# The first chunk of a gated delta-rule recurrence, begun inside the triangular solve ahead of it

## The chip, the cores and the metric

One core of a Trainium2 chip runs the kernel. The metric is the device time of one execution in microseconds; the kernel before was run three times, and its median is the time before. On the core, TensorE (PE in the profile) multiplies matrices, VectorE (DVE) and ScalarE (ACT) do the elementwise work and copy results out of PSUM, GpSimd (POOL) does some small work, and SyncE (SP) issues most of the transfers. Engines wait for each other by semaphores.

## What is computed

The reference is one transformer layer over 2048 tokens of width 512: a layer norm, then a gated delta-rule attention and a feed-forward part whose weights are spline-interpolated. Only the attention's recurrence matters here; per token and head (6 heads, keys of 64, values of 128):

```python
def _step(S, xs):
    qt, kt, vt, gt, bt = xs
    S = S * jnp.exp(gt)[..., None, None]
    pred = jnp.einsum('bhk,bhkv->bhv', kt, S)
    delta = (vt - pred) * bt[..., None]
    S = S + jnp.einsum('bhk,bhv->bhkv', kt, delta)
    return (S, jnp.einsum('bhk,bhkv->bhv', qt, S))
```

The kernel doesn't go token by token. For a chunk of 128 tokens all deltas U come from one triangular system: U = W (V - gamma K S), with W an inverse that doesn't depend on the state S, and K S the product of the chunk's keys with the state at its start.

## The kernel before, in words

The function `attend` computes the attention, `feed` the feed-forward part behind it. `attend` goes over 4 supersteps of 512 tokens, each of 4 chunks of 128 tokens (NCH = 4). One superstep has a part that needs no state (`local`: projections, convolutions, scores, and at its end `solve`, which puts together the inverse W of each chunk) and a part that does (`recur`, once for each chunk). On TensorE, `recur` of superstep r stands behind `solve` of superstep r, and the projections of superstep r+1 behind that.

Every engine has its own program, written out by hand; what keeps them in step are the eight PSUM banks. `bank_uses` (line 163) lists every use of every bank in order. `claim` (547) makes TensorE wait until the use before in this bank has been read out; `filled` (528) makes a reader wait until TensorE has written it; `ready` (533) makes anyone wait until the reader is done. The change leaves `bank_uses` as it is.

`solve` on TensorE (650) is a pipeline of seven steps, k = 0 to 6. Step k holds, in this order: a transpose of values (`v_transposes(k + 1)`, for k = 1 to 4), X of chunk k (line 660), Y and Z of chunk k-1 (670, 676), and, interleaved, X2 of chunk k-2 (691) and Z2 of chunk k-3 (696). So the fifth step (k = 4) has the last transpose, Y and Z of chunk 3, X2 of chunk 2 and Z2 of chunk 1; the sixth has X2 of chunk 3 and Z2 of chunk 2; the seventh has Z2 of chunk 3 alone. All Z2 lie in bank 6, all X2 in bank 7, so the Z2 of one chunk can be made only once that of the chunk before has been copied out.

VectorE's `solve` (1006) copies out X (1012), Y (1019), Z (two instructions, 1024) and Z2 (1031), in that order within a step. ScalarE (1309 to 1315) goes through, for c = 0 to 3: `v_tokens(c + 2)`, which copies a transposed block of values out into V in four pieces (1246), and the copy of X2 of chunk c (1314). Its last `v_tokens` (for head 5) thus stands behind the copy of X2 of chunk 2.

`recur` on TensorE (710) makes, for chunk c: KS, the keys times the state, in two halves of three heads (706); U, with the inverse, in two halves (722), once VectorE's `right_sides` (1034, the six instructions of line 1041) has made V - gamma K S out of KS; QS, the queries times the state (706 too, in banks 6 and 7); dS, the state's increment (733); AU (740). VectorE's `state` (1051) then updates S, for which the next chunk's KS waits. KS lies in banks 2 and 3, U in banks 4 and 5. A matmul of float32 shows as two records.

## Time and profile before

| | us |
|---|---|
| median of 3 runs | 1062.36 (1059.04 to 1064.06) |
| span of the profiled execution, first to last instruction | 1047.6 |
| TensorE busy | 904.7 |
| VectorE busy | 632.2 |
| ScalarE busy | 456.8 |
| GpSimd busy | 331.9 |
| mean granted clock of TensorE, share of full speed | 0.922 |

The profiled execution's whole duration isn't given, only its span; the median stands 14.8 us above that. The span is one hardware-profiled execution; the runs are others. A row of a timeline gives the start and the duration of an instruction, or of several like ones in a row (x12), and in brackets how long its engine had been idle and who released it. The part with the feed-forward network starts at about 700 us and isn't touched.

### The profile page before, as it was taken

The numbers are of one execution on the slowest core, as the hardware profiler recorded it, in microseconds if no ns is written. First come the engines' busy times: TensorE is split into PE (matmuls) and PEld (weight loads), VectorE is DVE, ScalarE is ACT, GpSimd is POOL, SyncE is SP. The second block draws the span as 40 slices with busy tenths as digits, with TensorE's granted clock in tenths as the row PEclk, the third lists the DMA queues.
The fourth block names the chain that finished last, engine by engine and source line by source line (L and its number), as shares of the span: only waits on it lengthen the run. The fifth ranks groups of instructions, "written<-read, shape, count | busy, mean of one in ns | idle before, by whom it ended". The sixth has DMA issues, their size and how long they took to land. (4 is left out here: it accounts for less than half of the span.)

```text
span 1047.6 us, 16055 instructions
## 1 busy us (share of the span) xinstructions
PE 904.7 (86%) x5976; PEld 527.2 (50%) x5976; DVE 632.2 (60%) x1447; ACT 456.8 (44%) x1038; POOL 331.9 (32%) x348
## 2 busy tenths in 40 slices
PE   3788298989798989798989798667699999999888
PEld 1453187555486555486555486322344444444333
DVE  5889656676656676656676645359892291390530
ACT  3645335445635535635435634245771170260420
POOL 2477601165701265701265701079060000000000
PEclk9999689989979989979989979967899999999999
DMA  6322310101410101410101300160552102101101
GB/s 203 136 61 58 67 36 21 71 1 31 81 52 21 71 1 31 81 52 21 71 1 31 81 12 21 45 225 0 208 174 71 50 1 80 41 0 40 40 21 41
DMA packets 70543, 61.61 MB, mean 59 GB/s; under 512 B 48059, under 2 KB 52028, under 8 KB 70470
## 3 DMA queue, kind: packets, MB, share of 16 engines
q1 hardware_dynamic: 62526, 41.42, 13.9%
q0 software_dynamic: 4224, 13.37, 4.0%
q10 hardware_dynamic: 3720, 5.85, 1.6%
q8 instruction: 45, 0.74, 0.3%
q14 instruction: 28, 0.23, 0.1%
HBM read 38.08 MB, written 23.13 MB: 58 GB/s over the span
## 5 line engine op out<-in xcount | busy, mean ns | idle before, releaser
L1924 ACT ACTIVATE sg<-pg 128x512 f32<-128x512 f32 x64 | 37.6, 590 | 147.6 <-PE pg L1825 147.5
L2040 DVE SCALAR_TENSOR_TENSOR yr<-pd,yr 128x512 f32<-128x512 f32 x16 | 11.1, 691 | 146.4 <-PE pd L1836 146.4
L1834 PE MATMUL pd<-dw,it 128*128 128x512 f16 x256 | 97.1, 379 | 1.5 <-DVE it L2035 1.5
L1835 PE MATMUL pd<-dw,it 128*128 128x512 f16 x256 | 97.1, 379 | 0.0
L1836 PE MATMUL pd<-dw,it 128*128 128x512 f16 x256 | 97.1, 379 | 0.0
L1734 POOL DMA_DIRECT2D yr<-y_attn x16 | 8.7, 544 | 239.4 <-DMA out<-yr 239.4
L559 PE MATMUL bank<-x_hi,w_hi 128*128 128x512 f16 x192 | 73.7, 384 | 2.7 <-DVE x_lo L866 1.5
L559 PE MATMUL bank<-x_lo,w_hi 128*128 128x512 f16 x192 | 73.5, 383 | 0.0
L559 PE MATMUL bank<-x_hi,w_lo 128*128 128x512 f16 x192 | 73.3, 382 | 0.0
L559 PE MATMUL bank<-w_hi,x_hi 128*128 128x384 f16 x128 | 44.4, 347 | 23.9 <-ACT gate L1207 15.4
L1407 POOL TENSOR_TENSOR rn<-t,mhalf 128x6 f32<-128x6 f32 x16 | 22.6, 1415 | 128.1 <-DVE t L1066 128.1
L1798 PE MATMUL pf<-fx_hi,b_hi 128*128 128x512 f16 x128 | 52.3, 408 | 0.7 <-DVE f L1989 0.7
L2031 DVE TENSOR_TENSOR hh<-sg,pu 128x512 f32<-128x512 f32 x64 | 43.9, 687 | 14.3 <-ACT sg L1924 9.6
L909 DVE SCALAR_TENSOR_TENSOR cv<-raw,taps,cv 128x512 f32<-128x512 f32 x72 | 52.3, 791 | 0.0
L1799 PE MATMUL pf<-fx_lo,b_hi 128*128 128x512 f16 x128 | 52.1, 407 | 0.0
L1800 PE MATMUL pf<-fx_hi,b_lo 128*128 128x512 f16 x128 | 51.4, 402 | 0.0
L706 PE MATMUL bank<-S,kq 64*128 64x128 f32 x384 | 48.0, 321 | 4.0 <-DVE BA L1062 3.7
L950 DVE SCALAR_TENSOR_TENSOR BA<-bank,cj,eg 128x256 f32<-128x256 f32 x96 | 39.0, 474 | 18.1 <-PE bank L639 15.1
L989 DVE TENSOR_TENSOR bank<-bank,tin 96x60 f32<-96x60 f32 (+32 forms) x184 | 46.6, 281 | 2.3
L1340 ACT ACTIVATE junk<-BA 128x128 bf16<-128x128 f32 x96 | 28.6, 298 | 42.5 <-DVE BA L1062 42.4
L995 DVE TENSOR_TENSOR tin<-tin,bank 96x60 f32<-96x60 f32 (+32 forms) x184 | 45.4, 272 | 2.2
L706 PEld LDWEIGHTS bank<-S,kq 64*128 64x128 f32 x384 | 41.4, 215 | 9.0 <-issue 7.2
(249 smaller groups left out, 2300.7 us busy)
## 6 DMA issues: line engine op xcount, KB each, us to landing
xb<-in_x SPq DMA_DIRECT2D x4, 1024.0 KB, 5.7
xr<-in_x SPq DMA_DIRECT2D x16, 256.0 KB, 2.8
y_attn<-xr SPq DMA_DIRECT2D x16, 256.0 KB, 2.5
down_rows<-dn SPq DMA_DIRECT2D x4, 1024.0 KB, 7.8
yr<-y_attn POOLq DMA_DIRECT2D x16, 256.0 KB, 2.8
out<-yr SPq DMA_DIRECT2D x16, 256.0 KB, 2.0
xn_hi<-x_hi POOLq DMA_DIRECT2D x4, 512.0 KB, 3.1
xn_lo<-x_lo POOLq DMA_DIRECT2D x4, 512.0 KB, 4.5
```

What stands on the lines that cost most here:

```text
L559: ins = nc.tensor.matmul(out, a, b, start=first and i == 0, stop=last and i == 2)
L706: ins = nc.tensor.matmul(ps[:, 128 * (h // 2):128 * (h // 2) + 128], kq[rows, h // 2, which, CH * c:CH * c + CH], P.S[rows, h // 2, :], st ...
L909: ins = v.scalar_tensor_tensor(out=out, in0=src, scalar=w, in1=out, op0=ALU.mult, op1=ALU.add)
L989: done_to[k] = step(v.tensor_tensor(prod, row.unsqueeze(2).broadcast_to([NINST, n, c1 - c0]), tv[:, j, c0:c1].unsqueeze(1).broadcast_to([N ...
L995: done_to[k] = step(v.tensor_tensor(rest, rest, prod, ALU.subtract))
L1798: nc.tensor.matmul(ps[:], f_h, x_hi[:, hb, :], start=hb == 0, stop=False)
L1799: nc.tensor.matmul(ps[:], f_h, x_lo[:, hb, :], start=False, stop=False)
L1800: ins = nc.tensor.matmul(ps[:], f_l, x_hi[:, hb, :], start=False, stop=hb == HB - 1)
L1834: nc.tensor.matmul(ps[:], it_hi[:, i, tok], dw[:, i, 0, :], start=i == 0, stop=False)
L1835: nc.tensor.matmul(ps[:], it_hi[:, i, tok], dw[:, i, 1, :], start=False, stop=False)
L1836: ins = nc.tensor.matmul(ps[:], it_lo[:, i, tok], dw[:, i, 0, :], start=False, stop=i == IB - 1)
L2031: v.tensor_tensor(hh[:, i % 2, :], sg[:, i % 2, :], pu[i % 2][:], ALU.mult).then_inc(h_ready, 1)
```

## The change

KS of chunk 0 is made inside `solve`, its first half ahead of the fifth step's Y, its second half behind the fifth step's Z. VectorE makes the right sides of chunk 0 in its own fifth step, behind the copies of Z and ahead of the copy of Z2 of chunk 1, and waits for the last values (`("vtr", NV - 1)`) first. U of chunk 0 is made behind the sixth step. `recur` of chunk 0 begins with QS. Chunks 1 to 3 are as before; the functions `state_product` and `right_sides` are only moved up, and `solved_sides` is the part of `recur` that makes U.

```diff
+            def solved_sides(s, c):
+                ready(pe, ("Z2", c), s)
+                for hf in range(2):
+                    ps, f = claim(("U", c, hf), s)
+                    ready(pe, ("KS", c, hf), s)
+                    for h in range(hf, NH, 2):
+                        ins = nc.tensor.matmul(ps[:, 128 * (h // 2):128 * (h // 2) + 128], W[:, ch(c, h), :], Rr[:, h, :], start=True, stop=True)
+                    ins.then_inc(f, 1)
+
             def solve(s):
...
+                    if k == NCH:
+                        state_product(s, 0, "KS", 0, 0)
                     c = k - 1
                     if 0 <= c < NCH:
...
+                    if k == NCH:
+                        state_product(s, 0, "KS", 0, 1)
                     c, c2 = k - 2, k - 3
...
+                    if k == NCH + 1:
+                        solved_sides(s, 0)
 
             def recur(s, c):
                 if c >= 1:
                     ready(pe, ("dS", c - 1), s)
-                for hf in range(2):
-                    state_product(s, c, "KS", 0, hf)
-                if c >= 2:
-                    project_out(s, c - 2)
-                ready(pe, ("Z2", c), s)
...
+                    for hf in range(2):
+                        state_product(s, c, "KS", 0, hf)
+                    if c >= 2:
+                        project_out(s, c - 2)
+                    solved_sides(s, c)
                 for hf in range(2):
                     state_product(s, c, "QS", 1, hf)
...
                             ins = v.tensor_scalar(W[r:r + SUB, mine, r + SUB:r + 2 * SUB],
                                                   heads64(ps, slice(r, r + SUB))[:, :, SUB:], -1.0, None, ALU.mult)
                         ins.then_inc(d, 1)
+                    if k == NCH:
+                        ready(dve, ("vtr", NV - 1), s)
+                        right_sides(s, 0)
                     c = k - 3
                     if 0 <= c < NCH:
                         filled(dve, ("Z2", c), s)
...
             def recur(b, c, following=None):
-                right_sides(b, c)
+                if c >= 1:
+                    right_sides(b, c)
                 if following is not None and c == 0:
                     ln_tile_stats(following)
```

## Rows read from the trace of the kernel before

Rows 7 and 8 are tables by stretch; their columns are: stretch, its length, then busy time and count for TensorE, its weight loads, VectorE, ScalarE and GpSimd, then the granted TensorE clock as a share of full speed, the busy share of the transfers' engines and GB/s.

**Rows 1.** From the page: span, busy time of the engines, TensorE clock in 40 slices

```profile
span 1047.6 us, 16055 instructions
...
PE 904.7 (86%) x5976; PEld 527.2 (50%) x5976; DVE 632.2 (60%) x1447; ACT 456.8 (44%) x1038; POOL 331.9 (32%) x348
...
PEclk9999689989979989979989979967899999999999
```

**Rows 2.** Timeline of ACT, last solve: start, duration, line, operation

```profile
614.27 0.48 ACT L1314 ACTIVATE X2s<-bank 64x384 f32<-64x384 f32 x1 [1.01 <-PE bank L691]
614.78 1.14 ACT L1246 ACTIVATE V<-bank,nk 128x128 f32<-128x128 f32 x4
```

**Rows 3.** Timeline of DVE, last solve, and the right sides of the first chunk

```profile
613.76 0.71 DVE L1024 TENSOR_SCALAR W<-bank 32x192 f32<-32x192 f32 x2 [0.17 <-PE bank L676]
614.50 0.55 DVE L1031 TENSOR_SCALAR W<-bank 64x384 f32<-64x384 f32 x1
...
618.84 1.64 DVE L1041 SCALAR_TENSOR_TENSOR BA<-bank,ngam,V 128x128 f32<-128x128 f32 x6 [0.52 <-PE bank L706]
```

**Rows 4.** Timeline of PE, last solve, from its first step to its seventh

```profile
598.36 1.55 PE L660 MATMUL bank<-Tbd,BA 64*64 64x64 f32 x24 [4.04 <-DMA Tbd<-t_blocks]
599.83 1.11 PE L647 MATMUL bank<-ident,vT 128*128 128x128 f32 x4
...
602.21 1.38 PE L670 MATMUL bank<-eg,W 64*64 64x64 f32 x11
...
605.38 0.92 PE L660 MATMUL bank<-Tbd,BA 64*64 64x64 f32 x24
...
615.26 0.24 PE L691 MATMUL bank<-T,BA 64*64 64x64 f32 x1 [1.03 <-DVE W L1031]
...
616.83 0.91 PE L696 MATMUL bank<-W,X2s 64*64 64x64 f32 x12 [0.65 <-DVE W L1031]
```

**Rows 5.** Timeline of PE, last superstep, first chunk

```profile
617.66 1.77 PE L706 MATMUL bank<-S,kq 64*128 64x128 f32 x12
619.85 2.90 PE L722 MATMUL bank<-BA,W 128*128 128x128 f32 x12 [0.42 <-DVE BA L1041]
622.68 2.24 PE L706 MATMUL bank<-S,kq 64*128 64x128 f32 x12
624.85 1.55 PE L733 MATMUL bank<-BA,ktok 128*64 128x128 f32 x12
626.33 2.63 PE L740 MATMUL bank<-BA 128*128 128x128 f32 x12
```

**Rows 6.** Timeline of PE, last superstep, second chunk

```profile
628.88 1.72 PE L706 MATMUL bank<-S,kq 64*128 64x128 f32 x12
630.87 1.70 PE L722 MATMUL bank<-BA,W 128*128 128x128 f32 x12 [0.26 <-DVE BA L1041]
632.49 1.26 PE L706 MATMUL bank<-S,kq 64*128 64x128 f32 x12
...
635.55 0.88 PE L733 MATMUL bank<-BA,ktok 128*64 128x128 f32 x12
636.36 1.61 PE L740 MATMUL bank<-BA 128*128 128x128 f32 x12
```

**Rows 7.** One microsecond each, last superstep: busy time by engine, then clock, DMA

```profile
618.00:619.00 1.00, 1.00 (x11) 1.00 (x10) 0.48 (x2) 0.00 (x0) 0.00 (x0) 0.63 0.00 0
...
628.00:629.00 1.00, 1.00 (x7) 0.88 (x7) 0.56 (x1) 0.32 (x2) 0.00 (x0) 0.75 0.00 0
```

**Rows 8.** Same columns, 14 us from the sixth step of each solve

```profile
145.00:159.00 14.00, 11.50 (x102) 10.34 (x104) 7.99 (x24) 4.47 (x15) 1.02 (x1) 0.76 0.00 1
301.00:315.00 14.00, 12.55 (x96) 11.21 (x96) 7.30 (x24) 4.07 (x13) 0.09 (x1) 0.63 0.00 1
458.00:472.00 14.00, 12.62 (x96) 11.21 (x96) 7.54 (x24) 4.00 (x13) 0.40 (x1) 0.63 0.00 1
```

**Rows 9.** The line that evacuates Z2: who waited for it, in total us, times

```profile
  PE bank L691: 4.2, 4
```

More of the change, by code:

```diff
@@ L648, in v_transposes, with state_product @@
                 ins.then_inc(f, 1)
+            def state_product(s, c, name, which, hf):
+                ps, f = claim((name, c, hf), s)
+                for h in range(hf, NH, 2):
+                    rows = slice(DK * (h % 2), DK * (h % 2) + DK)
+                    ins = nc.tensor.matmul(ps[:, 128 * (h // 2):128 * (h // 2) + 128], kq[rows, h // 2, which, CH * c:CH * c + CH],
+                                           P.S[rows, h // 2, :], start=True, stop=True)
+                ins.then_inc(f, 1)
[4 more added lines that the diff above has]
+                    ready(pe, ("KS", c, hf), s)
+                    for h in range(hf, NH, 2):
+                        ins = nc.tensor.matmul(ps[:, 128 * (h // 2):128 * (h // 2) + 128], W[:, ch(c, h), :], Rr[:, h, :], start=True, stop=True)
+                    ins.then_inc(f, 1)
             def solve(s):
@@ L699, in solve @@
                                 ins.then_inc(f2, 1)
-            def state_product(s, c, name, which, hf):
-                ps, f = claim((name, c, hf), s)
-                for h in range(hf, NH, 2):
-                    rows = slice(DK * (h % 2), DK * (h % 2) + DK)
-                    ins = nc.tensor.matmul(ps[:, 128 * (h // 2):128 * (h // 2) + 128], kq[rows, h // 2, which, CH * c:CH * c + CH],
-                                           P.S[rows, h // 2, :], start=True, stop=True)
-                ins.then_inc(f, 1)
+                    if k == NCH + 1:
+                        solved_sides(s, 0)
             def recur(s, c):
@@ L712, in recur @@
                     ready(pe, ("dS", c - 1), s)
-                for hf in range(2):
-                    state_product(s, c, "KS", 0, hf)
-                if c >= 2:
-                    project_out(s, c - 2)
-                ready(pe, ("Z2", c), s)
-                for hf in range(2):
-                    ps, f = claim(("U", c, hf), s)
-                    ready(pe, ("KS", c, hf), s)
-                    for h in range(hf, NH, 2):
-                        ins = nc.tensor.matmul(ps[:, 128 * (h // 2):128 * (h // 2) + 128], W[:, ch(c, h), :], Rr[:, h, :], start=True, stop=True)
-                    ins.then_inc(f, 1)
+                    for hf in range(2):
[3 more added lines that the diff above has]
+                    solved_sides(s, c)
                 for hf in range(2):
@@ L998, in invert_blocks, with right_sides @@
                 step(v.tensor_copy(bin_[:].rearrange("p (c i) -> p c i", c=SUB), tin[:].rearrange("p (i c) -> p c i", i=SUB)))
+            def right_sides(s, c):
+                for hf in range(2):
+                    u = ("KS", c, hf)
+                    filled(dve, u, s)
+                    ps, d = out_of(u)
+                    for h in range(hf, NH, 2):
+                        ins = v.scalar_tensor_tensor(out=Rr[:, h, :], in0=ps[:, 128 * (h // 2):128 * (h // 2) + 128],
+                                                     scalar=ngam[:, ch(c, h):ch(c, h) + 1], in1=V[:, c, h, :],
+                                                     op0=ALU.mult, op1=ALU.add)
+                    ins.then_inc(d, 1)
             def heads3(ps):
@@ L1032, in solve @@
                                         ALU.mult).then_inc(d, 1)
-            def right_sides(s, c):
-                for hf in range(2):
-                    u = ("KS", c, hf)
-                    filled(dve, u, s)
-                    ps, d = out_of(u)
-                    for h in range(hf, NH, 2):
-                        ins = v.scalar_tensor_tensor(out=Rr[:, h, :], in0=ps[:, 128 * (h // 2):128 * (h // 2) + 128],
-                                                     scalar=ngam[:, ch(c, h):ch(c, h) + 1], in1=V[:, c, h, :],
-                                                     op0=ALU.mult, op1=ALU.add)
-                    ins.then_inc(d, 1)
             def state(s, c):
```

## The prediction

> **What bounds the kernel now.** I read the page first, then the granted clock, then the timelines of the three engines around one solve. TensorE is busy for 86% of the span and its clock dips once in each superstep [rows 1]; the mean hides that the stretch which the change touches isn't a stretch of full matrices. It is a relay: TensorE makes a small product, VectorE or ScalarE copies it out, and TensorE's next step waits for that copy. In the last solve VectorE finishes the masked copies of Z at 614.47 and the copy of Z2 for chunk 1 at 614.50 + 0.55 = 615.05 [rows 3]; TensorE stands idle for 1.03 us and starts the sixth step at 615.26, put down to that very copy; the seventh waits 0.65 us for the next one [rows 4]. All four solves do it: TensorE waited for that line 4.2 us in 4 waits, 1.05 each [rows 9]. Behind the solve come, on TensorE one after the other, the key products KS (617.66), the product U with the inverse (619.85), the query products QS (622.68), the state's increment dS (624.85), AU (626.33) and the next chunk's KS (628.88) [rows 5, 6]. I use the start of that last one as the finish line: what it moves by, each superstep moves by, since every later chunk hangs on this one and the feed part starts only behind the last.
>
> The second thing to see is the clock. It is at its upper level (2.4 GHz) through the solve, falls to 1.2 GHz in the microsecond from 618 (0.63, so at about 618.3) and is back in the one from 628 (0.75, so at about 628.5) [rows 7]. The three other supersteps show the same dip (means of 0.76, 0.63 and 0.63 over 14 us) [rows 8]. U, QS, dS and AU of the first chunk take 2.90, 2.24, 1.55 and 2.63 us in it [rows 5] against 1.70, 1.26, 0.88 and 1.61 in the second chunk at the upper level [rows 6].
>
> **The change, part by part.** No instruction is added or taken away; twelve matmul records (KS) and six vector operations (1.64 us) per superstep move ahead, and one wait is added. No DMA and nothing on GpSimd or SyncE moves. I walk the last superstep, as its rows are complete.
>
> *KS into the fifth step.* KS costs 1.26 us at the upper clock (the like-shaped QS) [rows 6] where it took 1.77 [rows 5]. But it stands ahead of the product X2 of chunk 2, so X2 and Z2 of that step end 1.26 us later. ScalarE's copy of X2 moves from 614.27 to 615.53 [rows 2]. This price is certain: the products run in the order in which they are written.
>
> *The new wait.* VectorE's right sides need V of chunk 0 for all heads, so it now waits for the last V transposes to be copied out. On ScalarE that copy (four pieces, 1.14 us) stands behind the X2 copy: 614.78 before [rows 2], so 615.53 + 0.51 = 616.04 now, done at 617.18. This is the crux. TensorE made that transpose at the head of the fifth step; it is ScalarE's order that keeps it back.
>
> *What is queued behind the wait.* On VectorE, first the six right sides: 617.24 to 618.88 (1.64 us) [rows 3]. Then the copy of Z2 of chunk 1, which was ready all along: to 618.88 + 0.55 = 619.43 instead of 615.05. TensorE's sixth step claims the same bank and waits for it. With the old hand-over (615.05 to 615.26, 0.21) it starts at 619.64 instead of 615.26: 4.4 us later, and TensorE idles for about 4.1 us where it idled for 1.03.
>
> *What is given back.* The sixth step's 24 small products, then U at once (its inputs are long ready), then the seventh step, whose wait is now hidden under U, then QS. Gone are the old KS between solve and U (617.66 to 619.85, 2.2 us with the 0.42 us wait for the first right sides [rows 5]) and the 0.65 us. New is a wait ahead of QS: it needs the bank of the last Z2, which VectorE can empty only behind the seventh step: 0.04 + 0.55 + 0.2, about 0.8 us.
>
> *At which clock.* The clock already falls at 618.3 with gaps of 1.03 and 0.65 us before it; with one of 4.1 us in the same place I take it to fall at the same time, so that everything from the sixth step on runs at the lower level. Durations there: 24 small products 1.47 (598.36 to 599.83) against some 0.75 at the upper one (0.92 less the tail of the last); the twelve of Z2, between 0.83 (616.83 to 617.66, mostly at the upper level) and 1.38 (eleven of the like-shaped Y at the lower), take 1.25 [rows 4, 5]. So: sixth step 619.64 to 621.1; U 2.83 to 623.95; Z2 to 625.2; wait to 626.0; QS 2.17 to 628.2; the clock rises at 628.5 as before, in dS, which ends at 629.15; AU about 1.55 to 630.7. KS of chunk 1 starts at 630.7 instead of 628.88: 1.8 us later. For four supersteps, taken as equal: 7.3 us.
>
> The clock's own terms are the unknown ones; their bounds, by the same walk. With the upper level throughout: sixth step to 620.4, U (1.62) 622.0, Z2 (0.83) 622.85, wait 623.65, QS (1.19) 624.85, dS (0.81) 625.65, AU (1.55) 627.2: a gain of 1.7 us. With a rise only behind AU: QS 628.2, dS (1.48) 629.7, AU (2.8) 632.5: a loss of 3.6 us. I take the value between, whose fall and rise are those of the rows.
>
> *A rule against the trace.* The profile shows short gaps behind nothing but vector copies, and the clock down 1.6 us after the second [rows 4, 7]. The Trainium skill ("TensorE: Matmul & The Clock Gate", the section "Loop structure matters more than you think") says that a VectorE copy out of PSUM between bursts of matmuls doesn't cost the engine its warmth, and that a long wait for a DMA does. Were that so here, the upper-level walk would hold (rival 3 below); in this trace the clock fell behind just such copies.
>
> *Switches of the array's shape.* The moved products put 64x128 tiles between 64x64 ones, twice more per superstep. Going from Z2 (64x64) to KS shows 0.07 us of overlap and no idle [rows 4, 5]: between 0 and 0.2 us each, taken as 0. The skill's "TensorEngine Tiling (Array Packing)", section "Key Properties", says that a change of tiling mode drains the engine; by it the sum would be longer, by less than the bound here.
>
> The sum is made on the profiled execution. Its span is 1047.6 us [rows 1]; its whole duration isn't given; the median of the three runs lies 14.8 us above the span, which I leave as it is. 1062.4 + 7.3 = 1069.7, so 1070.
>
> **The rivals.**
> 1. *Late rise.* The longer gap also keeps the clock down through AU: four times 3.6, 14.4 us: 1077. For it: the gap is four times as long, and a second one of 0.8 us follows. Against: U, then at 128x128, keeps TensorE dense for 2.8 us.
> 2. *Early rise.* The clock comes back ahead of QS, near 625.5: QS 1.19 to 627.2, dS 628.0, AU 629.55, so 0.7 us later per superstep: 1065. For it: the first superstep's dip is the shortest (mean 0.76) [rows 8].
> 3. *The clock stays up: faster.* The inserted KS keeps TensorE dense in the fifth step, and the copies' gap doesn't bring the clock down before U is through. Price: minus 1.7 four times, 6.8 us: 1056. The point from which it decides is whether U is still at 2.4 GHz. Against: all four dips of today follow shorter gaps.
> 4. *The wait costs nothing.* If the V copy were done when VectorE asks for it (by 615.10, the end of the Z copies of today plus the 0.63 us of the first KS half), the right sides would end at 616.8, Z2's copy at 617.35, and TensorE would start the sixth step at 617.6, 2.3 us later instead of 4.4; the walk then ends 0.3 us ahead of today's at the lower clock: 1061. Against: ScalarE's order, by which the copy can't begin before X2 of chunk 2 is out.
>
> **How the numbers follow.** Forecast 0.60; late rise 0.13; early rise 0.14; clock stays up 0.07; wait free 0.06. The predicted time is the likeliest case's, 1070. Its own range, with the runs' spread of 5 us (1059.0 to 1064.1), is 1066 to 1074. For eight in ten I go down past the early rise to 1062, the edge of the free wait, and up to the late rise, 1077; outside lie the stay-up case and tails. About 0.5% (5.3 us) is what a measurement of this kernel tells from no change: the line is at 1067.7. Of the forecast case three quarters and more lie above it (0.48), of the late rise all (0.13): slower 0.62 with a little of the early rise. Faster by 0.5% needs the clock up nearly throughout: 0.05. The same: 0.33.
>
> **What would show it.** In the changed profile, right sides (line moved into the solve) should start 3 us after the Z copies end, with the V copy as the releaser; TensorE's sixth step should show about 4 us idle ahead of it; no gap before U; 0.8 us before QS; granted clock at 1.2 GHz from U on in all four dips. The forecast is wrong if TensorE's gap is under 2 us, if U runs in 1.7 us, or if the dip ends before QS. The sum is mis-sized where the next KS starts by other than 1.8 us later than now, counted from the start of the solve's fifth step.

## The result, and the profile after

| | before | changed |
|---|---|---|
| median of the timed runs, us | 1063.2 (4 runs, 1059.0 to 1065.8) | 1074.3 (4 runs, 1072.6 to 1076.3) |
| ratio to before | | 1.0138 (95%: 1.0100 to 1.0177) |
| the same on another chip (29 and 6 runs), us | 1046.5 | 1063.4, ratio 1.0159 (1.0127 to 1.0190) |
| span of the profiled execution, us | 1047.6 | 1071.9 |

The change makes the kernel slower, as forecast, but by more: 11.1 us between the medians (16.8 on the other chip) where the sum had 7.3. The profiled execution of the changed kernel took 1073.5 us for a span of 1071.9, so only 1.6 us lie around a span; the 14.8 us between the span and the median of before were no fixed part: the profiled execution of before was simply quicker than the timed ones, in the feed part, as further looks show below. The ratio on record, 1.0138, stands for 14.7 us, twice the sum, and is a little higher than that of the medians, 1.0104; the four runs listed for the kernel before don't show why. Ratios rest on fast runs alone: runs more than 1.5% above the fastest of their kernel are left out, which were one of 1504.3 us at a granted clock of 0.556 (right sides behind Z2) and two of the kernel before without its feed part.

The page of the changed kernel, in the lines of [rows 1]:

```profile
span 1071.9 us, 16059 instructions
...
PE 915.2 (85%) x5976; PEld 527.2 (49%) x5976; DVE 627.5 (59%) x1447; ACT 457.7 (43%) x1038; POOL 327.2 (31%) x348
...
PEclk9989689989889979999989889767889999999999
```

TensorE, last superstep: start, duration, line, operation. Line 655 makes KS and QS, 690 Y, 696 Z, 713 X2, 665 U, 718 Z2, 742 dS, 749 AU.

```profile
617.48 0.93 PE L655 MATMUL bank<-S,kq 64*128 64x128 f32 x6
618.34 0.85 PE L690 MATMUL bank<-eg,W 64*64 64x64 f32 x11
...
619.09 0.86 PE L696 MATMUL bank<-W,eg 64*64 64x64 f32 x23
619.88 0.93 PE L655 MATMUL bank<-S,kq 64*128 64x128 f32 x6
...
625.68 0.34 PE L713 MATMUL bank<-T,BA 64*64 64x64 f32 x1 [4.03 <-DVE W L1055]
...
627.16 2.93 PE L665 MATMUL bank<-BA,W 128*128 128x128 f32 x12
630.02 1.01 PE L718 MATMUL bank<-W,X2s 64*64 64x64 f32 x12
631.67 1.26 PE L655 MATMUL bank<-S,kq 64*128 64x128 f32 x12 [0.64 <-DVE W L1055]
632.87 0.88 PE L742 MATMUL bank<-BA,ktok 128*64 128x128 f32 x12
633.67 1.60 PE L749 MATMUL bank<-BA 128*128 128x128 f32 x12
635.42 1.51 PE L655 MATMUL bank<-S,kq 64*128 64x128 f32 x12
```

These answer [rows 4, 5]. KS stands ahead of Y (617.48) and behind Z (619.88). The sixth step begins at 625.68 after 4.03 us of idle time, released by VectorE's copy of Z2 (line 1055), where it was 1.03 us. U starts behind the sixth step with no gap and takes 2.93 us, at the lower clock. QS waits 0.64 us for the last Z2, then takes 1.26 us, and dS 0.88: the upper clock again.

VectorE and ScalarE in the same stretch, answering [rows 3] and [rows 2]:

```profile
620.00 0.71 DVE L1045 TENSOR_SCALAR W<-bank 32x192 f32<-32x192 f32 x2 [0.17 <-PE bank L696]
623.38 1.64 DVE L1016 SCALAR_TENSOR_TENSOR BA<-bank,ngam,V 128x128 f32<-128x128 f32 x6 [2.66 <-ACT V L1259]
624.93 0.54 DVE L1055 TENSOR_SCALAR W<-bank 64x384 f32<-64x384 f32 x1
...
631.07 0.55 DVE L1055 TENSOR_SCALAR W<-bank 64x384 f32<-64x384 f32 x1 [3.24 <-PE bank L718]
```

```profile
621.69 0.49 ACT L1327 ACTIVATE X2s<-bank 64x384 f32<-64x384 f32 x1 [3.04 <-PE bank L713]
622.20 1.14 ACT L1259 ACTIVATE V<-bank,nk 128x128 f32<-128x128 f32 x4
```

The Z copies end at 620.71. The right sides (line 1016) start at 623.38 after 2.66 us of idle time, released by ScalarE's copy of V; that copy starts only behind the copy of X2 (621.69). Z2 of chunk 1 comes last, done at 625.47. TensorE's clock (stretch, length, busy times of five engines, then the clock), answering [rows 7]:

```profile
623.00:624.00 1.00, 0.00 (x0) 0.00 (x0) 0.62 (x3) 0.34 (x2) 0.00 (x0) 0.73 0.00 0
630.00:631.00 1.00, 1.00 (x13) 0.88 (x12) 0.00 (x0) 0.49 (x1) 0.00 (x0) 0.86 0.00 0
```

It falls in the gap itself, at about 623.5, and is back at about 630.3, behind U: 6.8 us at 1.2 GHz where it was 10.2.

### The profile page after: what moved, and what is told of

Read it like the earlier page. It is cut to its first block and busy times, and to the rows that moved or that the text cites. A ratio compares the mean times of both kernels' runs of the same rounds, so it can differ in the third digit from the quotient of the medians.

```text
span 1071.9 us, 16059 instructions
## 1 busy us (share of the span) xinstructions
PE 915.2 (85%) x5976; PEld 527.2 (49%) x5976; DVE 627.5 (59%) x1447; ACT 457.7 (43%) x1038; POOL 327.2 (31%) x348
## 3 DMA queue, kind: packets, MB, share of 16 engines
q1 hardware_dynamic: 62526, 41.42, 13.6%
## 5 line engine op out<-in xcount | busy, mean ns | idle before, releaser
L2053 DVE SCALAR_TENSOR_TENSOR yr<-pd,yr 128x512 f32<-128x512 f32 x16 | 11.1, 692 | 148.1 <-PE pd L1849 148.1
L559 PE MATMUL bank<-w_hi,x_hi 128*128 128x384 f16 x128 | 44.6, 348 | 21.1 <-ACT gate L1220 12.6
L2044 DVE TENSOR_TENSOR hh<-sg,pu 128x512 f32<-128x512 f32 x64 | 43.9, 688 | 22.3 <-ACT sg L1937 11.8
L655 PE MATMUL bank<-S,kq 64*128 64x128 f32 x384 | 43.4, 288 | 8.9 <-DVE BA L1074 5.9
L559 PE MATMUL bank<-w_hi,x_lo 128*128 128x384 f16 x128 | 44.7, 349 | 0.0
```

Of the source, the lines that this page charges most:

```text
L559: ins = nc.tensor.matmul(out, a, b, start=first and i == 0, stop=last and i == 2)
L655: ins = nc.tensor.matmul(ps[:, 128 * (h // 2):128 * (h // 2) + 128], kq[rows, h // 2, which, CH * c:CH * c + CH], P.S[rows, h // 2, :], st ...
L2044: v.tensor_tensor(hh[:, i % 2, :], sg[:, i % 2, :], pu[i % 2][:], ALU.mult).then_inc(h_ready, 1)
```

## Experiments

The table sets the traces of all kernels with a feed part side by side. The stretches are worked out from TensorE's timelines: A is from the start of the solve's fourth X to the next chunk's first KS, summed over four supersteps (81.2 us before); B from there to the start of the superstep's last AU, summed; C from the first superstep's fourth X to the first product of the feed part; D from there to the end of the span. "Low" is the time at 1.2 GHz in the 50 us behind each fourth X, from the granted clock of one-microsecond stretches, summed over four.

| kernel | A | B | C | D | low | ratio to before (95%) |
|---|---|---|---|---|---|---|
| before | 81.2 | 132.2 | 547.3 | 361.7 | 40.9 | |
| before, second look | 80.5 | 131.7 | 548.5 | 374.2 | 37.4 | 0.9996 (0.9964 to 1.0028) |
| before, third look | 78.1 | 132.5 | 543.9 | 371.1 | 34.0 | |
| changed | 88.2 | 134.1 | 558.4 | 376.8 | 30.6 | 1.0138 (1.0100 to 1.0177) |
| changed, second look | 88.2 | 134.1 | 557.4 | 364.5 | 30.6 | 1.0159 (1.0127 to 1.0190) |
| changed, third look | 87.8 | 134.1 | 555.8 | 372.5 | 27.2 | |
| V copied ahead of X2 | 71.8 | 133.5 | 538.2 | 374.5 | 13.6 | 0.9972 (0.9937 to 1.0008) |
| right sides behind Z2 | 76.8 | 132.8 | 538.0 | 374.5 | 17.0 | 0.9958 (0.9929 to 0.9988) |
| both edits | 68.1 | 131.9 | 530.1 | 375.1 | 3.4 | 0.9935 (0.9903 to 0.9968) |
| changed, gap filled | 81.1 | 132.1 | 541.7 | 362.3 | 6.8 | 1.0020 (0.9997 to 1.0042) |
| KS alone moved | 82.9 | 135.7 | 552.3 | 363.0 | 40.8 | 1.0068 (1.0048 to 1.0089) |
| before, V ahead of X2 | 80.2 | 132.1 | 543.8 | 362.5 | 34.0 | 0.9993 (0.9970 to 1.0016) |
| before with the wait alone | 91.7 | 133.2 | 560.3 | 372.3 | 58.0 | 1.0196 (1.0127 to 1.0265) |
| before, gaps filled | 69.8 | 133.5 | 534.3 | 378.2 | 10.2 | 0.9957 (0.9922 to 0.9992) |
| changed, layer-norm work moved | 85.7 | 131.8 | 551.5 | 364.4 | 27.2 | 1.0067 (1.0040 to 1.0093) |
| both edits and that | 64.7 | 132.9 | 532.4 | 365.2 | 3.4 | 0.9914 (0.9881 to 0.9946) |

My theory going in was that of the prediction: VectorE's new wait holds the copy of Z2 of chunk 1, TensorE stands, and its clock falls. The rivals: that the moved KS products cost the time, that the wait is only a symptom, and that the rest of the loss lies in the feed part.

### The kernel before, looked at again

> The kernel before, unchanged, looked at a second time. The profile of before spans 1047.6 us, 24.3 us less than that of the changed kernel (1071.9), while the timed runs differ by 11.1 us. Theory A: the attention part of that profile is typical and only its feed part was quick (361.7 us from the first feed product to the end, against 376.8 us in the changed kernel, whose code there is the same); then the feed part takes about 375 us here, the first feed product comes at 686 +- 3 us, and the span is about 1061 us. Theory B: the feed part was typical and the change slows it; then the span is again near 1048 us. Time in both: equal to before, ratio 1.00.

Theory A: C is 548.5 us and D 374.2. The feed part has two kinds of duration, and they go with the chip in these traces: on the second chip, that of this run, 374.2 to 375.1 in four traces of four kernels; on the third 362.3 to 364.5 in four others. Which chips the first two profiles (361.7 and 376.8) came from isn't on record. Of the 24 us between the first two spans 11 lie in C, where the change is, and 15 in D, less 2 ahead of both.

### The V copy ahead of X2

```diff
                 for c in range(NCH):
-                    v_tokens(s, c + 2)
+                    if c < NCH - 1:
+                        v_tokens(s, c + 2)
+                    if c == NCH - 2:
+                        v_tokens(s, NV - 1)
                     u = ("X2", c)
```

> The changed kernel with ScalarE's last copy of V put ahead of its copy of X2 of chunk 2, so that VectorE's new wait is over when it comes to it. Theory A (the wait behind ScalarE's order is over half of the stall): TensorE's gap ahead of the sixth step falls from 4.03 us to about 2.0 us, the right sides start right behind the Z copies, the next chunk's KS starts some 2 us sooner per superstep than in the changed kernel, 8 us in all: 1065 us, level with before within 3 us. Rival B (the right sides themselves, 1.64 us ahead of the copy of Z2, and not the wait, are what counts): the gap stays above 3 us and the time at 1072 or more.

TensorE's gap ahead of the sixth step, and U behind it, last superstep:

```profile
606.67 0.24 PE L713 MATMUL bank<-T,BA 64*64 64x64 f32 x1 [1.41 <-DVE W L1055]
...
607.76 2.93 PE L665 MATMUL bank<-BA,W 128*128 128x128 f32 x12
```

The gap is 1.41 us, under the 2.0 that I expected, and A falls by 16 us, twice what I had written: 0.9972 of before, which its interval can't tell from no change. Theory A holds, and its 8 us were too few, because the clock gains too: the time at the lower level falls from 30.6 to 13.6 us. Rival B falls.

### The right sides behind the copy of Z2

```diff
-                    if k == NCH:
-                        ready(dve, ("vtr", NV - 1), s)
-                        right_sides(s, 0)
                     c = k - 3
                     if 0 <= c < NCH:
...
                                         ALU.mult).then_inc(d, 1)
+                    if k == NCH:
+                        ready(dve, ("vtr", NV - 1), s)
+                        right_sides(s, 0)
```

> The changed kernel with the right sides behind the copy of Z2 of chunk 1 instead of ahead of it; the wait for V stays. Theory A (what costs is that this copy is queued behind the wait): the gap ahead of the sixth step falls from 4.03 us to about 0.8 us; a new one of 1 to 1.3 us comes ahead of U, which now waits for the right sides (done 1.7 us behind the sixth step). The next KS then comes within 0.3 us of where it comes in the kernel before if the clock falls as it does there, and 3 us sooner if it stays up: 1063 us, down to 1055. Rival B (the stall comes from elsewhere, the KS products or the moved order of the banks): still 1070 or more.

```profile
611.23 0.24 PE L713 MATMUL bank<-T,BA 64*64 64x64 f32 x1 [0.84 <-DVE W L1052]
...
613.12 1.68 PE L665 MATMUL bank<-BA,W 128*128 128x128 f32 x12 [0.98 <-DVE BA L1016]
```

The wait is still there, but nothing that TensorE needs at once is queued behind it: 0.84 us ahead of the sixth step, 0.98 ahead of U for the right sides, as theory A has it. 0.9958: faster than before, by a little.

### Both edits: a version that beats both kernels

> Both edits: V copied ahead of X2, and the right sides behind the copy of Z2 of chunk 1. Theory A: no gap above 1 us is left between the fifth step and QS but the 0.7 us for the last Z2; the sixth step starts 1.1 us later than in the kernel before (the moved KS), U follows it at once, and the next KS comes 1.6 us sooner than before per superstep at the lower clock and up to 5 us sooner at the upper: 1057 us, down to 1045. Rival B (the clock takes it all back, falling for longer because less idle time is left in which nothing was lost anyway): 1062 to 1065.

The sixth step, U and QS of the last superstep, then 20 us of it as a stretch (the clock is the third number from the end):

```profile
602.22 0.24 PE L713 MATMUL bank<-T,BA 64*64 64x64 f32 x1 [0.84 <-DVE W L1052]
...
603.06 1.60 PE L665 MATMUL bank<-BA,W 128*128 128x128 f32 x12
...
606.15 1.26 PE L655 MATMUL bank<-S,kq 64*128 64x128 f32 x12 [0.64 <-DVE W L1052]
```

```profile
600.00:620.00 20.00, 16.02 (x180) 14.01 (x180) 11.46 (x36) 9.29 (x33) 1.33 (x1) 1.00 0.00 1
```

Only 0.84 and 0.64 us of gaps are left ahead of QS and the clock stays at its upper level in three supersteps of four; U takes 1.60 us. A is 68.1 us, 11.8 less than the mean of the three looks at before (79.9). Timed it is 0.9935, clear of no change; the 1057 us expected were 0.994 of the 1063.2 us then known. So the idea of the change is sound, and its place in two queues is what undid it.

### The changed kernel again, beside the kernel before

> The changed kernel, unchanged, timed again beside the kernel before on one chip, as the first comparison rests on four runs of each, and the kernel before varies by 14 us from run to run. Theory A (the walk: 1.9 us per superstep up to the next chunk's KS, as the trace of the changed kernel shows, 7 us in all, and nothing more): ratio 1.007, within 0.003. Theory B (there is a further loss of 4 to 7 us behind that point, in the rest of the recurrence or in the feed part): ratio 1.011 to 1.015, and the trace again shows 1 us or more per superstep lost between that KS and the next solve.

1.0159, with 1.0127 at the low end: theory B. A is 7 us above the first look at before, as the walk had it, and the rest is behind it: B 134.1 against 132.2, C 557.4 against 547.3.

### The gap filled with idle products

```diff
+                    if k == NCH + 1:
+                        ps, _ = claim(("U", 0, 0), s)
+                        for _ in range(14):
+                            nc.tensor.matmul(ps[:, 0:128], P.after[:], P.upto[:], start=True, stop=True)
                     c, c2 = k - 2, k - 3
```

> The changed kernel with its 4.03 us gap ahead of the sixth step filled by 14 idle products (128x128 by 128, float32, constants, about 3.7 us at the upper clock) into the bank that U overwrites later. All that waits, waits as long. Theory A (half of what the change costs is TensorE's clock, which falls in that gap): the clock stays up through the gap and U, U takes 1.6 us instead of 2.8, the next KS comes at 19 us behind the start of the fourth X instead of 22.1, 3 us sooner per superstep, 12 us in all: ratio to before 0.995. Rival B (the clock falls for the whole region whatever fills the gap, or the products get in the way of the others): ratio above 1.005.

The idle products (line 704), the sixth step, U, and the clock of the 20 us around them:

```profile
611.41 3.39 PE L704 MATMUL bank<-upto,after 128*128 128x128 f32 x28
615.50 0.24 PE L717 MATMUL bank<-T,BA 64*64 64x64 f32 x1 [0.70 <-issue]
...
616.35 1.60 PE L665 MATMUL bank<-BA,W 128*128 128x128 f32 x12
```

```profile
610.00:630.00 20.00, 17.08 (x188) 15.28 (x188) 9.08 (x29) 9.78 (x36) 1.33 (x1) 1.00 0.01 2
```

Every wait of the changed kernel is still there, yet the clock stays up, U takes 1.60 us and A falls from 88.1 (mean of three looks) to 81.1, by 1.7 us per superstep instead of the 3 expected. The 19 us expected are reached in the last superstep alone (19.24); in the three others the next KS waits some 1.3 us for VectorE, which has the next superstep's layer norm in between, as it does in the changed kernel unfilled. The ratio is 1.0020 against 1.0159 on the same chip: filling the gap gives back 1.4 points, where theory A had 0.995. C falls by more than A (541.7 against 557.2), by 2 us in B and 6.5 us in the rest, the projections. Why, no run here shows. What this run can't say is how much of the change's loss is the clock's, for the kernel before has dips of its own; the run that fills those is below.

### KS alone moved

```diff
-                    if k == NCH + 1:
-                        solved_sides(s, 0)
...
-                    if k == NCH:
-                        ready(dve, ("vtr", NV - 1), s)
-                        right_sides(s, 0)
```

with the right sides and U of chunk 0 back in `recur`.

> Only the KS products of chunk 0 go into the fifth step; the right sides stay behind the solve on VectorE, U stays in the recurrence, and no wait for V is added. Theory A: the sixth step starts 1.26 us later than in the kernel before behind an unchanged gap of 1.03 us, the right sides can start right behind the copy of the last Z2 or of the one before, U starts about 0.5 us behind the seventh step's end; the next KS comes 0.3 to 0.6 us sooner at an unchanged clock (ratio 0.998), and 3 us sooner where the clock now stays up (ratio 0.99). Rival B (the moved products themselves delay the solve and give nothing back): next KS 1 us later, ratio 1.004.

```profile
620.61 0.24 PE L713 MATMUL bank<-T,BA 64*64 64x64 f32 x1 [0.84 <-DVE W L1050]
...
624.59 2.66 PE L665 MATMUL bank<-BA,W 128*128 128x128 f32 x12 [1.51 <-DVE BA L1014]
```

Neither number was right: 1.0068. The sixth step still waits only 0.84 us, but U waits 1.51 us for right sides that start only behind the last Z2 copy. A is 3.0 us above the mean of before, B 3.6 us above: rival B, less than its 1 us per superstep in A, more behind it. Moving the products without the work that reads them gives nothing back, and the clock is down as long as in the first look at before (40.8 us).

### ScalarE's order alone, in the kernel before

> The kernel before with only ScalarE's order changed: the last copy of V ahead of the copy of X2 of chunk 2. A control for the two runs with that edit. Theory A (that order matters only through the new wait): X2 of chunk 2 is copied up to 0.2 us later or not at all, every gap of the solve is as before, ratio 1.000 within 0.003, and the clock falls for 10 us in each superstep as before. Rival B (the order by itself speeds the solve up): a smaller gap ahead of the sixth step, ratio 0.997 or less.

0.9993 within 0.0023: theory A. The order matters only through the new wait.

### The new wait alone, in the kernel before

```diff
+                    if k == NCH:
+                        ready(dve, ("vtr", NV - 1), s)
                     c = k - 3
                     if 0 <= c < NCH:
                         filled(dve, ("Z2", c), s)
```

> The kernel before with nothing moved, only the new wait put in: VectorE waits for the last copy of V before it copies out Z2 of chunk 1. Theory A (the wait alone is worth its time on the path): V is copied out at +1.65 us behind X2, so the copy of Z2 ends 1.5 us later, TensorE's gap ahead of the sixth step is 2.5 us instead of 1.03, and the next KS comes 1.5 us later per superstep at an unchanged clock: 6 us, ratio 1.006. Rival B (part of it is taken back because the clock's dip is shorter, as in the changed kernel): ratio 1.002. Rival C (a longer gap makes the dip longer): 1.010 or more.

The sixth step, U, and 20 us of the last superstep:

```profile
624.48 0.24 PE L691 MATMUL bank<-T,BA 64*64 64x64 f32 x1 [2.47 <-DVE W L1033]
...
630.21 2.90 PE L722 MATMUL bank<-BA,W 128*128 128x128 f32 x12 [0.46 <-DVE BA L1043]
```

```profile
623.00:643.00 20.00, 17.15 (x120) 15.40 (x120) 7.00 (x21) 6.27 (x25) 0.68 (x1) 0.66 0.00 1
```

This is the sharpest of the runs. One added wait, which moves nothing, costs 1.0196, as much as the whole change or more. The gap is 2.47 us as worked out (1.44 more than before), yet A grows by 3.0 us per superstep against the mean of before: the other half is the clock, 58.0 us at the lower level instead of 34 to 41. Rival C. The changed kernel has the longer gap (4.03 us) and a shorter time at the lower level (27 to 31 us): so the length of one gap doesn't set the length of the dip.

### The gaps of the kernel before filled

```diff
+                    if k > NCH:
+                        ps, _ = claim(("U", 0, 0), s)
+                        for _ in range(3 if k == NCH + 1 else 2):
+                            nc.tensor.matmul(ps[:, 0:128], P.after[:], P.upto[:], start=True, stop=True)
```

> The kernel before with its gaps of 1.03 and 0.65 us ahead of the sixth and seventh steps filled by 3 and 2 idle products (128x128 by 128, float32, 0.27 us each at the upper clock). Nothing else changes. Theory A (the clock's dip behind the solve comes from these two gaps and costs some 4 us per superstep): granted clock 1.00 through KS, U, QS, dS and AU, the next KS at 16 to 17 us behind the start of the fourth X instead of 20.3, ratio 0.985 to 0.99. Rival B (the dip has its cause in the products themselves, KS with half the array's rows, and not in the gaps): the dip stays, KS as late as before, ratio 1.000 to 1.002.

The idle products (line 682), U, and the clock of 20 us:

```profile
605.12 0.94 PE L682 MATMUL bank<-upto,after 128*128 128x128 f32 x6
...
607.06 0.71 PE L682 MATMUL bank<-upto,after 128*128 128x128 f32 x4
...
610.60 1.68 PE L726 MATMUL bank<-BA,W 128*128 128x128 f32 x12 [0.72 <-DVE BA L1045]
```

```profile
606.00:626.00 20.00, 16.61 (x168) 14.49 (x168) 10.59 (x34) 9.60 (x36) 1.33 (x1) 1.00 0.01 2
```

In the trace theory A's mechanism holds: clock 1.00 through the recurrence's first chunk, U 1.68 us instead of 2.90, the next KS at 17.4 us (mean of four) instead of 20.0, and C 12.3 us shorter than the mean of before. The 16 to 17 us expected came in the last superstep alone (16.3); in the other three the next KS waits 1.27 us for VectorE. Timed it is 0.9957, 4.5 us, not the 10 to 15 expected; this trace has the longest feed part of all (378.2 us, against 371.1 to 372.5 in three others of that chip), which would account for 6 us of the difference. Whether that is a habit of this kernel or one execution wasn't tried.

This run also says what the change costs where the clock is up on both sides. With its gap filled the changed kernel has 81.1 us in A and 541.7 in C; the kernel before with its gaps filled has 69.8 and 534.3. So 11.3 us are lost in A and 7.4 in C, against 8.1 and 10.6 unfilled; the ratios, 1.0020 and 0.9957, lie 0.6 points apart, on different chips and with the long feed part of this trace unexplained. By these two traces, one of each kernel, the change costs about 7 us with the clock up on both sides, so most of its loss is the stall itself and not the clock.

### Third looks at both, on one chip

> The kernel before, a third look. Theory A (the attention part of the kernel before takes 544 to 548 us from the start of the first solve's fourth X to the first feed product, the changed kernel 558, and the feed part has two durations, 362 and 375 us, which go with the chip and not with the kernel): 544 to 548 us here, and the same feed duration as the changed kernel beside it. Theory B (the change makes the feed part slower by 2 to 4 us): the two differ.

> The changed kernel, a third look, on the same chip as the third look at the kernel before. Theory A: attention part 558 us as in the two looks before (11 to 14 us more than the kernel before), feed part as beside it within 1 us. Theory B: feed part 2 to 4 us longer.

Single executions of 1055.4 and 1066.4 us: 11.0 apart. C differs by 11.9 us and D by 1.4, where 1 was allowed: theory A, nearly.

### Both kernels without the feed part

> The kernel before without its feed-forward part: the attention's result alone is copied to the output, so the feed part of the computation is left out. About 690 us. The difference to the changed kernel without the same part, over many runs, is the whole cost of the change in the attention part, free of the feed part's own spread (362 to 378 us in the traces). Theory A (all that the timed runs show lies in the attention part): difference 15 us. Theory B (the attention part loses 10.6 us, as the three traces of each show on average, and the rest is in the feed part or is spread): difference 10 to 11 us.

> The changed kernel without its feed-forward part, which is left out of the computation in the same way. Theory A: 15 us above the kernel before without it, so about 705 us. Theory B: 10 to 11 us above it. The walk of the prediction alone (7.3 us, up to the next chunk's KS) would give 7 to 8.

Medians of 691.1 us (six runs, 682.8 to 695.4) and 701.6 us (five, 700.6 to 704.6): 10.4 us apart. That would be theory B, but two of the six (693.8 and 695.4) are among the runs left out; the median of the four others is 687.8 us, 13.8 below 701.6. As ratios to the kernel before they are 0.6536 (0.6506 to 0.6565) and 0.6694 (0.6671 to 0.6717), 16 us apart by that reckoning; the means of all runs, 690.1 and 702.7, lie 12.6 apart. So these runs don't tell theory A (15 us) from theory B (10 to 11); they do put the loss in the attention part above the walk's 7 to 8. The traces have 10.6 us there (C: 546.6 and 557.2 on average). That the third chip's timed pair shows 16.8 us isn't explained: no look at the plain kernel before was taken on it.

### The layer-norm work moved out of the way

What was still open was why the attention part loses 10.6 us and the walk had 7.3. In the changed kernel's second superstep VectorE does this behind the solve (846 the statistics of the next superstep's layer norm, 855 to 861 its moments, 1063 the state, 1074 the outputs), and TensorE waits for the outputs before the next KS:

```profile
313.49 0.55 DVE L1055 TENSOR_SCALAR W<-bank 64x384 f32<-64x384 f32 x1 [3.36 <-PE bank L718]
313.96 2.45 DVE L846 BATCH_NORM_STATS2 stats<-xb 128x6 f32<-128x512 f32 x4
316.34 0.84 DVE L1063 SCALAR_TENSOR_TENSOR S<-S,gC,bank 128x128 f32<-128x128 f32 x3
317.11 0.15 DVE L855 TENSOR_TENSOR mv<-stats 128x4 f32<-128x4 f32 x1
...
318.30 0.16 DVE L861 SCALAR_TENSOR_TENSOR mv<-ln_d,mv 128x4 f32<-128x4 f32 x1
318.38 1.02 DVE L1074 TENSOR_TENSOR BA<-bank,BA 128x384 f32<-128x384 f32 x2
```

```profile
316.09 1.60 PE L749 MATMUL bank<-BA 128*128 128x128 f32 x12
319.08 1.30 PE L655 MATMUL bank<-S,kq 64*128 64x128 f32 x12 [1.38 <-DVE BA L1074]
```

In the first look at the kernel before the next KS waited 0.38 us or less in the second and third superstep, but 1.27 us in the first. Two supersteps of kernels whose right sides stand behind the solve, as before, show what makes the difference. The second superstep of the kernel before, its AU (740), the state's update and the next KS (706), at the lower clock:

```profile
312.57 2.50 PE L740 MATMUL bank<-BA 128*128 128x128 f32 x12
312.69 0.86 DVE L1051 SCALAR_TENSOR_TENSOR S<-S,gC,bank 128x128 f32<-128x128 f32 x3 [3.59 <-PE bank L733]
315.45 1.31 PE L706 MATMUL bank<-S,kq 64*128 64x128 f32 x12 [0.38 <-DVE BA L1062]
```

The same superstep of the kernel before with its gaps filled, at the upper clock (744 is AU, 710 KS):

```profile
304.57 1.61 PE L744 MATMUL bank<-BA 128*128 128x128 f32 x12
304.69 0.86 DVE L1055 SCALAR_TENSOR_TENSOR S<-S,gC,bank 128x128 f32<-128x128 f32 x3 [0.72 <-PE bank L737]
307.45 1.30 PE L710 MATMUL bank<-S,kq 64*128 64x128 f32 x12 [1.27 <-DVE BA L1066]
```

In both VectorE is done with the statistics and waits for dS; then the state, the moments (1.3 us) and the first half of the outputs stand against AU on TensorE. An AU at the lower clock (2.50 us here) hides them, one at the upper clock (1.6 us) doesn't. This goes through all traces in which the layer-norm work isn't moved. Of the three supersteps of each that have such work, where the clock was at its lower level for 5.4 us or more between the end of U and the end of AU, the next KS waited 0.00 to 0.38 us; where it was so for 1.5 us or less, 1.27 or 1.28 us with the right sides behind the solve and 1.32 or 1.38 with them moved. In the third superstep of the run with the right sides behind Z2 a long dip covers QS, dS and AU, and the wait is 0.

```diff
+                    if c == NCH - 1 and following is not None:
+                        ln_tile_stats(following, range(4))
                     if 0 <= c < NCH:
                         filled(dve, ("Z2", c), s)
...
-                if following is not None and c == 0:
-                    ln_tile_stats(following)
...
-                state(b, c)
                 if following is not None and c == 0:
                     ln_moments(following)
+                state(b, c)
```

> The changed kernel with the next superstep's layer-norm work taken out of VectorE's way: the four statistics go ahead of the copy of the last Z2 (VectorE is idle there for 3.4 us), the seven small steps of the moments (1.3 us) ahead of the state's update (2 us idle) instead of behind it. In the first three supersteps of the changed kernel the next KS waits 1.32 to 1.38 us for VectorE's outputs, which stand behind these steps; in the kernel before, at the lower clock, 0.38 us or less. Theory A (the change took the cover from this work, and a part of the loss beyond the walk is here): that wait falls below 0.5 us, A by 1 us per superstep in three of four, 3 us in all, C from 557 to 554, ratio about 0.003 lower, 1.011 to 1.013. Rival B (the wait for KS is only exchanged for one in the second chunk, or the clock takes it): C and ratio unchanged, 1.014 to 1.016.

AU and the next KS of the same superstep:

```profile
313.33 1.60 PE L749 MATMUL bank<-BA 128*128 128x128 f32 x12
315.08 1.51 PE L655 MATMUL bank<-S,kq 64*128 64x128 f32 x12
```

The wait of 1.38 us is gone. Theory A's effect holds, and goes further than I had it: 1.0067 where 1.011 to 1.013 was expected. A falls by 2.4 us against the mean of the changed kernel's looks, and B by 2.3: it is 131.8, what the kernel before has, and no later fall of the clock is left in any of the four supersteps. C is 551.5, 4.9 us above before, and the medians are 6.3 us apart (1053.6 and 1047.3), near the 7.3 of the walk. Two things are left open: this is one trace, and the kernel before with the same work moved wasn't run. Its next KS waited for VectorE too, 1.8 us per execution on the mean of three looks against 4.1 in the changed kernel, so up to some 2 us of this gain might be had there as well.

> The version with both edits (0.9935 of before, V copied ahead of X2 and right sides behind the copy of Z2) with the same layer-norm work moved: two statistics ahead of the last Z2's copy, two behind it, the moments ahead of the state's update. Theory A: the next KS waits 0.5 us instead of 1.38 in three supersteps, A falls by some 2.5 us to 65.5, ratio 0.990 to 0.992. Rival B: as without the move, 0.9935.

0.9914 (0.9881 to 0.9946), medians of 1036.2 and 1047.3 us: as theory A has it, and the lowest ratio of the study, though its interval overlaps that of both edits alone (0.9903 to 0.9968), so rival B isn't excluded. The next KS waits 0.26 to 0.33 us in the three supersteps; one of them still shows a later fall of the clock, 3.4 us long.

## What the prediction had right, and the steps that failed

Forecast were 1070 us, 1066 to 1074 in the likeliest case and 1062 to 1077 for eight in ten; measured are 1074.3.

**The chain: right, step for step.** ScalarE's order held back V (right sides 2.66 us after the Z copies, 3 forecast), the right sides and then the copy of Z2 followed, TensorE stood for 4.03 us (4.1 forecast), U followed the sixth step without a gap, and 0.64 us (0.8) came ahead of QS. The runs that mend either queue take the loss away, and the one that adds the wait alone makes it.

**KS in the fifth step: 1.26 us in the sum, 2.0 measured.** From the start of the fourth X, ScalarE's copy of X2 starts at 7.57 us (614.12 to 621.69) instead of 5.53 (608.74 to 614.27). Each half takes 0.86 us to the next product (Y starts at 618.34 behind 617.48, X2 at 620.74 behind 619.88), not 0.63, and X2 no longer starts under the tail of Z, which is worth another 0.3. I had bounded the switches of shape at 0 to 0.2 us each and taken 0; that was too low. The sixth step came 5.04 us later, not 4.38. The tiling rule of the Trainium skill that I had set aside ("TensorEngine Tiling (Array Packing)", "Key Properties": a change of mode drains the engine) points the right way: 0.78 us more than the products' own 1.26. That a drain is what took it, no run here tests.

**The clock: the forecast's fall and rise were wrong, rival 2 came true.** I had the dip end in dS as before, and had named a dip that ends before QS as a sign that the forecast is wrong. It ended behind U, so QS, dS and AU ran at 2.4 GHz: the walk of rival 2, 0.7 us, plus the 0.66 of the line above gives 1.4; the last superstep lost 1.16 (21.30 us against 20.14 from the fourth X). The mean loss in stretch A over all looks is 2.0 us per superstep (88.1 against 79.9 for four), against 1.8 in the sum: close by luck, as the costlier KS and the wait of the next paragraph make up for the early rise. The clock ahead of this was misread as well: it was not at its upper level all through the last solve of the kernel before but at 1.2 GHz from about 597.8 to 604.6, ahead of the point from which I count, so no term hangs on it.

**The step that failed: four supersteps "taken as equal", and the finish line.** I walked only the last superstep, "as its rows are complete". It is the one superstep that has no layer norm to do. In the other three VectorE has the moments (1.3 us) between the state and the outputs, for which the next KS waits. With QS, dS and AU at the upper clock nothing hides them: the KS of the second chunk, which my walk starts right behind AU, waited 1.3 to 1.4 us in all nine such supersteps of the three looks, 4.1 us per execution, where the kernel before waited 1.8 (1.27 us in three of nine, those with a shorter dip). So what the early rise gives back is taken by this wait: those three lost 2.5, 2.0 and 1.4 us up to the next KS in the first looks, the last 1.2. The move of the right sides isn't the cause, as kernels that don't move them have the wait too, shorter by 0.05 to 0.1 us.

The larger part of what was missing lies behind the finish line. I had assumed that all behind the next KS moves as a block and put nothing there; B grew by 2.0 us and the rest of C by 0.5, of the 3.3 us that C lost beyond the sum (10.6 against 7.3). B's growth is a further fall of the clock in a later chunk, 3.4 us long, in two of four supersteps of each look: B is 34.2 to 34.6 us in those and 33.2 to 33.4 in the changed kernel's others with layer norm. The kernel before shows such a fall in three of twelve, early in the second chunk. With the layer-norm work moved both the wait and these falls go: 1.0067, a loss of 5 to 6 us of the 10.6 to 11. That the wait brings on the later fall isn't shown: one changed superstep in each look has the wait and no such fall, and some other kernels have the fall without the wait. Why the timed pair on the third chip lost 16.8 us stays open.

**The price of the stall.** With the same stall and the gap filled the ratio is 1.0020; unfilled 1.0159. My rival 3 named that decision point (U at 2.4 GHz) and put 1056 us on it; the filled kernel comes out level with before, not ahead, and 7.4 us in C behind a kernel before whose gaps are filled too. The rule of the Trainium skill ("TensorE: Matmul & The Clock Gate", section "Loop structure matters more than you think"), that a VectorE copy out of PSUM between bursts doesn't cost TensorE its warmth, is contradicted twice here: by the dips of before, and by their going when the 1.03 and 0.65 us gaps are filled.

**The base.** I set the sum on a median 14.8 us above the span and called that what lies around it. It is 1.6 us; the rest was another execution.

## What to carry to other kernels

Before an operation is moved up a queue, look for what already stands ahead of its input in the queue of the engine that makes it, and for what will stand behind its wait in its own: here one copy that was ready stood behind a wait that wasn't over, and exchanging two entries in one queue turned 1 to 1.5% slower into level with before (ScalarE's) or 0.4% faster (VectorE's), in both 0.7%. Walk a repetition that has all the work, not the last one because it is the simplest to read: there another engine's work may be hidden only as long as TensorE runs at its lower clock. Where the clock dips at a place already, a new gap costs more than its length: the one run that adds nothing else lost 3.0 us for 1.44. And to price a stall apart from the clock, fill the gaps in both kernels, not in one.

## What the runs showed of the hardware

- Gaps of 1.03 and 0.65 us between short bursts went with 6.8 to 10.2 us at 1.2 GHz in the 50 us behind, in every superstep of the kernel before; with 0.84 and 0.64 us, in the version with both edits, one dip of 3.4 us came in four supersteps. Filling the gaps of before with five idle products ended nearly all of it (34 to 41 us down to 10).
- A gap of 2.47 us was followed by 13.7 us at the lower level (in one superstep of four 10.2 and 3.4), one of 4.03 us by a dip of 6.8 us or less: the longer gap had the shorter dip. What follows the gap differs too, as U stands right behind the sixth step in the second.
- 64x128 products put between 64x64 ones took 0.86 us per six records where a run of twelve takes 1.26, and ended the overlap of the products on either side.
- The same VectorE work held up TensorE by 1.27 to 1.38 us where the products beside it ran at the upper clock and by 0.38 us or less where they ran at the lower.
- The feed part, the same instructions in every kernel, took 362 to 365 us on two chips and 371 to 378 on two others.
